# Token gathers of a 64-expert MoE layer issued five experts ahead, and seven output products of the first block placed behind the last down projection

## The reference

```
xn = layernorm(x)
x  = x + attention0(xn) + moe(xn)
xn = layernorm(x)
x  = x + attention1(xn) + ffn(xn)
```

## Time and profile before

| | us |
|---|---|
| median of 3 runs | 608.41 |
| lowest, highest | 607.96, 609.22 |
| the profiled execution | 609.91 |
| its span, first to last instruction | 607.8 |

### The profile page before, as it was taken

The page is one execution under the profiler, slowest core; times in us unless marked ns, Lnnn a source line. Parts: engine busy times, 40 slices in busy tenths (PEclk is TensorE's granted clock), DMA queues, the critical chain, the costliest instruction groups (busy, mean ns, idle before and its releaser), DMA issues.

```text
span 607.8 us, 9582 instructions
## 1 busy us (share of the span) xinstructions
PE 454.2 (75%) x2800; PEld 298.8 (49%) x2800; DVE 368.5 (61%) x960; ACT 200.1 (33%) x529; POOL 257.4 (42%) x237
## 2 busy tenths in 40 slices
PE   3846843287888888878878878889489989647866
PEld 1622513145455555545545545458234767536645
DVE  4999999544544444444443554532659867667984
ACT  1545220053334443343433334420165303021122
POOL 3331860215655665555665565632102043022444
PEclk9876985569888888898888999989689999788998
DMA  8430553628887878887887788733400287666502
GB/s 304 163 140 1 163 177 62 201 66 209 203 201 189 213 190 208 208 230 185 204 220 185 197 213 227 192 73 90 173 1 1 52 184 109 107 117 135 133 3 69
DMA packets 60579, 91.09 MB, mean 150 GB/s; under 512 B 23608, under 2 KB 39320, under 8 KB 60120
## 3 DMA queue, kind: packets, MB, share of 16 engines
q1 hardware_dynamic: 47656, 69.51, 41.0%
q0 software_dynamic: 12896, 21.24, 18.0%
HBM read 71.81 MB, written 18.12 MB: 148 GB/s over the span
## 4 chain that ended last, share of the span: by engine, by line
PE 26%; DMA 25%; issue 18%; DVE 15%; POOL 10%; ACT 4%; SPq 1%; ACTq 0%; POOLq 0%; DVEq 0%
PE ps L1431 19%; DMA big<-tok_tab,big 13%; DMA routed<-big 6%; POOL routed L655 6%; DMA big<-kr_dram 4%; POOL big L648 3%; DVE big L1409 3%; PE ps L1436 3%; DVE big L1046 2%; DVE big L1043 2%; DVE big L1050 1%; ACT big L810 1%; DMA big<-in_maa 1%; PE ps L1726 1%; PE ps L1743 1%
## 5 line engine op out<-in xcount | busy, mean ns | idle before, releaser
L1431 PE MATMUL ps<-big 128*128 128x352 f32 (+4 forms) x768 | 228.0, 448 | 2.3 <-ACT big L800 0.9
L1431 PEld LDWEIGHTS ps<-big 128*128 128x128 f32 (+2 forms) x768 | 150.9, 204 | 59.3 <-issue 23.8
L655 POOL DMA_INDIRECT routed<-big x64 | 101.8, 1591 | 127.2 <-ACT big L810 110.2
L648 POOL DMA_INDIRECT big<-tok_tab,big x64 | 63.5, 992 | 42.1 <-DVE big L1117 22.9
L1436 PE MATMUL ps<-cst,big 128*128 128x128 f32 x144 | 30.6, 301 | 57.9 <-DMA big<-tok_tab,big 56.5
L1139 DVE COPY big<-ps 88x256 f32<-88x256 f32 x64 | 26.9, 420 | 76.4 <-PE ps L1550 74.6
L1131 DVE SCALAR_TENSOR_TENSOR big<-big,ps 128x176 f32<-128x176 f32 x64 | 21.6, 338 | 78.3 <-ACT big L805 78.3
L1431 PE MATMUL ps<-xnT,big 128*128 128x512 f32 (+1 forms) x104 | 55.2, 690 | 14.8 <-ACT big L767 12.8
L800 ACT ACTIVATE big<-ps 128x256 f32<-128x256 f32 x64 | 24.5, 383 | 111.5 <-PE ps L1436 111.4
L1436 PEld LDWEIGHTS ps<-cst,big 128*128 128x128 f32 x144 | 17.7, 148 | 76.1 <-DMA big<-tok_tab,big 61.8
L1409 DVE TENSOR_TENSOR big<-ps,big 128x512 f32<-128x512 f32 x64 | 41.8, 677 | 9.3 <-PE ps L1726 9.3
(11 more groups left out here) (199 smaller groups left out, 679.7 us busy)
## 6 DMA issues: line engine op xcount, KB each, us to landing
big<-in_w SPq DMA_DIRECT2D x64, 352.0 KB
big<-in_w SPq DMA_DIRECT2D x64, 176.0 KB
big<-q_dram SPq DMA_DIRECT2D x144, 32.0 KB
big<-kr_dram SPq DMA_DIRECT2D x24, 192.0 KB
big<-kr_dram SPq DMA_DIRECT2D x72, 64.0 KB
big<-lo_tab SPq DMA_DIRECT2D x2, 2048.0 KB, 7.7
kr_dram<-big SPq DMA_DIRECT2D x12, 256.0 KB, 4.5
routed<-big POOLq DMA_DIRECT2D x2, 1152.0 KB, 14.1
```

The costliest lines, as they stand in the source:

```text
L648: nc.gpsimd.indirect_dma_start(xe[:, e % SLOTS, :], None, tok_tab, bass.IndirectOffsetOnAxis(ap=sidx[:, e:e + 1], axis=0))\
L655: nc.gpsimd.indirect_dma_start(routed[e % 2], bass.IndirectOffsetOnAxis(ap=sidx[:, e:e + 1], axis=0), ye[:, e % 2, :], None, compute_op=AL ...
L1431: last = nc.tensor.matmul(o, w, m, start=(n == 0), stop=(n == len(pairs) - 1))
```

## The change

- A small tile `gate_now` of 128x4 takes the gate column of each expert: `tokens_in` copies it on ACT ahead of its copy of the transposes, and `scale_out` reads it there. The slot of `xe` is so free once `tokens_in` of its expert is done.
- `token_gather(e)` therefore waits for `s_xeT` of expert e-4 and no longer for `s_y`. Five gathers are issued ahead of the loop, and in the loop `token_gather(e+5)` stands ahead of `routed_add(e)`.
- Of the output products only product 0 stays in the last group; products 1 to 7 follow the last down projection. DVE's adds are reordered around the additions of the `racc` halves, the statistics and the layernorm of half 0.
- SP issues the small rows of block 1 and `w5` ahead of the loads of `racc`, no longer behind them.

```diff
+        SLOTS = 4
+        gate_now = nat_tmp[:, 0, 0:SLOTS]
...
-        x1_at = [(), (), (0,), (1, 2, 3)]
+        x1_at = [(), (), (0,), ()]
...
             sp.wait_ge(s_lp, NG * 4)
+            sp.wait_ge(s_y, E + 1)
+            sp.dma_start(edrow, td_row.partition_broadcast(P)).then_inc(s_l1c, 16)
+            sp.dma_start(edcol, td_col).then_inc(s_l1c, 16)
+            sp.dma_start(urow, u_row.partition_broadcast(P)).then_inc(s_l1c, 16)
+            sp.dma_start(maat, maa).then_inc(s_l1c, 16)
+            sp.dma_start(w5, w_rkvgo).then_inc(s_w5, 16)
             for i in range(2):
                 sp.wait_ge(s_sc[i], 16 * (1 + E // 2))
                 for b in range(B):
                     sp.dma_start(racc[i][:, b * TPB:(b + 1) * TPB, :],
                                  routed[i][b * S:(b + 1) * S, :].rearrange("(t p) d -> p t d", p=P))\
                       .then_inc(s_racc[i][b], 16)
-            sp.wait_ge(s_y, E + 1)
-            sp.dma_start(w5, w_rkvgo).then_inc(s_w5, 16)
-            sp.dma_start(edrow, td_row.partition_broadcast(P)).then_inc(s_l1c, 16)
...
             def token_gather(e):
                 if e >= SLOTS:
-                    pool.wait_ge(s_y, e - SLOTS + 2)
+                    pool.wait_ge(s_xeT, e - SLOTS + 1)
...
-            for e in range(SLOTS):
+            for e in range(SLOTS + 1):
                 token_gather(e)
             for e in range(E):
+                if e + SLOTS + 1 < E:
+                    token_gather(e + SLOTS + 1)
                 routed_add(e)
-                if e + SLOTS < E:
-                    token_gather(e + SLOTS)
...
-            def tokens_in(e, u):
+            def tokens_in(e, u, gate):
                 act.wait_ge(s_xeTp, e + 1)
+                nc.scalar.activation(gate_now[:, u:u + 1], gate, ACT.Copy)
                 nc.scalar.activation(xeT[:, u % 2, :, :], PS[0][:, 0:D].rearrange("p (c n) -> p c n", c=DC),
                                      ACT.Copy).then_inc(s_xeT, 1)
...
-            def scale_out(e, u, free, gate):
+            def scale_out(e, u, free):
                 act.wait_ge(s_yp, e + 1)
+                act.wait_ge(s_xeT, e + 1)
                 act.wait_ge(s_sc[u % 2], free)
-                nc.scalar.activation(ye[:, u % 2, :], PS[3][:, 0:D], ACT.Copy, scale=gate).then_inc(s_y, 1)
+                nc.scalar.activation(ye[:, u % 2, :], PS[3][:, 0:D], ACT.Copy, scale=gate_now[:, u:u + 1])\
+                  .then_inc(s_y, 1)
...
-                        for t in range(3):
-                            x1_add(t)
+                        x1_add(0)
...
-            for t in range(3, TPB + 2):
+            for t in range(1, TPB):
                 x1_add(t)
-            dve.wait_ge(s_x1, TPB + 2)
+            dve.wait_ge(s_x1, TPB)
             routed_add(0, 0)
-            routed_add(0, 1)
+            x1_add(TPB)
             routed_add(1, 0)
             ln_stats(0)
-            for t in range(TPB + 2, NT):
+            for t in range(TPB + 1, TPB + 3):
                 x1_add(t)
-            dve.wait_ge(s_x1, NT)
-
+            ln_apply(1, 0)
             dve.wait_ge(s_ed, 2)
             note(nc.vector.tensor_scalar(edrow, edrow, 1e30, -1.0, ALU.min, ALU.mult))
             nc.vector.tensor_scalar(edcol, edcol, 1e30, -1.0, ALU.min, ALU.mult).then_inc(s_edn, 1)
-            ln_apply(1, 0)
+            x1_add(NT - 1)
+            dve.wait_ge(s_x1, NT)
+            routed_add(0, 1)
             routed_add(1, 1)
...
-            for t in range(4, NT):
+            for t in range(1, NT):
                 x1_product(t)
```

More of the change, by code:

```diff
@@ L421, in block_kernel @@
         LAST = NG - 1
-        x1_at = [(), (), (0,), (1, 2, 3)]
+        x1_at = [(), (), (0,), ()]
         oT_at = [(), (0, 1, 2), (3, 4, 5), (6, 7)]
-        SLOTS = 4
         KR_DMAS = PARTS + PARTS * PARTS
@@ L554, in _ @@
                       .then_inc(s_racc[i][b], 16)
-            sp.wait_ge(s_y, E + 1)
-            sp.dma_start(w5, w_rkvgo).then_inc(s_w5, 16)
-            sp.dma_start(edrow, td_row.partition_broadcast(P)).then_inc(s_l1c, 16)
-            sp.dma_start(urow, u_row.partition_broadcast(P)).then_inc(s_l1c, 16)
-            sp.dma_start(edcol, td_col).then_inc(s_l1c, 16)
-            sp.dma_start(maat, maa).then_inc(s_l1c, 16)
             sp.dma_start(gb[:, 0, :], gamma.partition_broadcast(P)).then_inc(s_gb, 16)
@@ L841, in unit @@
                 if g is not LAST or u + 2 < SLOTS:
-                    tokens_in(g * SLOTS + (u + 2), u)
-                scale_out(g * SLOTS + u, u, g * 32 + 16 * (1 + u // 2), gate)
+                    tokens_in(g * SLOTS + (u + 2), (u + 2) % SLOTS, gate)
+                scale_out(g * SLOTS + u, u, g * 32 + 16 * (1 + u // 2))
             def oT_copy(t):
@@ L853, in _ @@
             place_values(0, slice(0, 1), first=True)
-            tokens_in(0, 0)
+            tokens_in(0, 0, gates[:, 0, 0, 0:1])
             tanh(0, 0)
@@ L857, in _ @@
             exps(0, 1)
-            tokens_in(1, 1)
+            tokens_in(1, 1, gates[:, 1, 1, 0:1])
             with act.Fori(0, LAST) as g:
                 for u in range(SLOTS):
-                    unit(g, u, gates[:, u, u, bass.ds(g, 1)], bass.ds(g + 1, 1))
+                    n = (u + 2) % SLOTS
+                    unit(g, u, gates[:, n, n, bass.ds(g + (u + 2) // SLOTS, 1)], bass.ds(g + 1, 1))
             for u in range(SLOTS):
-                unit(LAST, u, gates[:, u, u, LAST:NG], None)
+                n = (u + 2) % SLOTS
+                unit(LAST, u, gates[:, n, n, LAST:NG], None)
             act.wait_ge(s_l1c, 64)
```

## The result

The changed kernel took 550.17 us in the median of 4 runs (548.33 to 556.54), against 608.18 us of the kernel before in the same runs: a ratio of 0.909, 95% interval 0.903 to 0.914. The direction was right, and its size was 34 us where 58 came.

The account below looks back on a forecast made before the run. Late gathers were taken to bound the expert loop, with DMA transfers next: 609.91 - 28.9 (loop) - 5 (end) = 576.0 us, less 1.5 for the median gives 574.5 us, range 557 to 598.

Parts of the forecast that it names:

- The gather ring: Expert loop: late gathers close a ring of four experts; issuing them earlier removes the gather wait entirely.
- Two experts more: POOL's queue in the loop: added gather lead of at least 2 x 3.2 us, against matmul waits of 2.6 at most.
- The transfers take over at a share of 0.92: 237 us: Expert loop: 218 us of full DMA share / 0.92 = 237 us, 28.9 us less.
- Rival 1: Expert loop: DMA share reaches 1.0 or over, only TensorE is left; 548 to 556 us in all; chance 0.11.
- Rival 2: Expert loop: uneven engines cap the mean DMA share at 0.84 to 0.88; 585 to 597 us in all; chance 0.20.
- Rival 3: Expert loop: scale_out waits for scatters landing in 6.7 us and over; 593 to 603 us in all; chance 0.06.
- rival 4: Loop gate copies cost 11 us while transfers already set the pace, end gives nothing back; about 618 us; chance 0.06.
- this floor: Loop scatters of one parity: scale_out(e) waits for scatter e-2 to land; 2.3 to 3.8 us an expert, 137 to 226 us.
- The end: 5 us: From the loop's end to block 1: first block-1 product 4.8 us earlier, taken as 5; bounds 1.7 to 8.
- the bound that I had worked out and put aside: SP queue at the end: w5, racc 0 and half 0, 2.9 MB, 11.8 us from 415.5, landing at 427.3.
- T: Landing of racc ring 1's half 0 load: forecast 424.2, before 427.75; first block-1 product then at T + 8.8.
- The clock rises: Expert loop: the mean clock rises above 0.92.

Follow-up runs that it names:

- the lead taken back: Changed kernel with the gather of e+4 behind the addition of e again, gate copies and new end kept: 611.29 us, ratio 1.011 against the kernel before.
- the three with late ones: The kernel before; that kernel with only the end reordered (606.32 us); the changed kernel with the gather of e+4 behind the addition of e (611.29 us).
- less work of TensorE: Changed kernel with half of each down product left out, 2 of 4 matmuls an expert: 551.95 us.
- fewer bytes: Changed kernel loading only 64 of the 512 columns of each w2 from the second group on: 547.51 us.
- the second one: Second profile of the changed kernel, run again unchanged on the chip of the other experiments: median 552.10 us.

## Why the prediction was wrong, point by point

1. *The gather ring bounds the loop, and its wait goes.* Right. With the lead taken back the loop is at 271 us, with it at 209 to 214.
2. *Two experts more lie between gather and use.* Right, and one would do.
3. *The transfers take over at a share of 0.92: 237 us.* This is the step that failed: 213.4 us measured, 23.6 less. (The total missed by 24.3: outside the loop 4 us of the extra gain were lost again, and the median lay 6.4 us below the profiled execution where 1.5 was assumed.) That they take over was right. The size was wrong in two ways. The share reached 0.96, and 0.98 over 38 us, above the 0.94 and 0.93 of the earlier trace rows, from which I even took a little off. And I took 0.82 x 265.86 = 218 us as a fixed amount of work. It is not: the same bytes (204 x 265.86 = 54.2 MB, 253 x 213.37 = 54.0 MB) took 0.96 x 213.37 = 205 us of full share after, 203 to 206 in the other loops with the same bytes and early gathers, but 218 to 220 in the three with late ones. With the share right and the 218 kept it would have been 218 / 0.96 = 227: 10 of the 24 us are the share, 14 the amount of work. Why the same bytes take less time of the engines is not shown. The stretches of the earlier trace rows gave 240 and 245 GB/s, and even from these alone it would have been 54.2 MB / 242 = 224 us.
4. *Rival 1, nothing but TensorE is left, 211 to 218 us and 548 to 556 in all.* Its numbers came true and its mechanism only in part: the share did rise to 0.96 and over, but TensorE was not all that was left, since less work of TensorE gave nothing and fewer bytes gave 6 to 10 us. That forecast and measurement meet in rival 1's total is in part luck. I gave it 0.11 because no long stretch before had a share over 0.94; but before, every such stretch ended in a hole of the kernel's own making, so the trace could not show a longer one.
5. *Rival 2, engines unevenly loaded, a cap at 0.84 to 0.88.* Wrong: the mean share was 0.96 to 0.98. The rule of the Trainium skill ("DMA: Bandwidth & Descriptors", "Why a DMA increments its semaphore by 16 and not by 1") on how many engines a narrow transfer uses was not tested by itself; if it holds here, it did not keep the mean down.
6. *Rival 3, late scatters, and rival 4, slower.* The output copy did wait for scatters, 10.2 us in 13 experts, which grew to 31.6 us in 28 with less TensorE, where it may be part of the bound. (By the earlier trace rows this floor is 2.2 to 3.7 us an expert, 134 to 224 us, not 137 to 226; nothing hangs on it.) Up to 6.8 us may be the gate copies where the gather is late, the piece of rival 4 that was real; in the changed kernel no cost of them could be seen, as the sum had it.
7. *The end: 5 us.* It was 2.5 us by the stages up to block 1 (-8.0 and +5.6). Scatter 63 came 1.5 us sooner than worked out (12.26 us behind scatter 60, for 13.8). But I let the load of half 0 land 3.85 us behind the scatter's landing; the queue set it, which was the bound that I had worked out and put aside: 13.7 us behind scatter 63 by that bound, 10.6 by the value taken, 15.2 measured. From T on the chain was right in this profile, T + 8.1 for T + 8.8 (T + 9.6 in the second one, at a clock of 0.65), and so was the new wait of x1_product(7) for VectorE.
8. *The clock rises.* Right: 0.92 to 0.99 in the loop, with 16 us less busy time for the same 957 matmul records.
9. *A measurement tells 0.2% from no change.* Wrong: the kernel before took 601.3 to 616.5 us over all runs, and the intervals of the ratios are 0.4% to 0.9% wide to either side.

## What to carry to other kernels

When a ring of latency is opened, the transfers that fill the holes can go faster than the mean of the trace with holes says, as here: work the new floor out from bytes and the best rate seen, not from the mean share times a guessed one, and put the case "the engines reach their full share" inside the range. A slot is free when its last reader is done: if that is a small part of the row (here one column of 320), copying it out early buys lead for the whole row, and the lead has to exceed the longest wait; here more of it gave nothing. And a load that is moved ahead in a queue is paid for by whatever stands behind it; here w5, needed much later, held the load that everything waited for back by 2.3 to 3.3 us, out of 8 that were won.

## What the runs showed of the hardware

The time that the 16 DMA engines spend on the same 54 MB is not constant. Over the stage from scatter 0 to scatter 60 the share times the length was 218 us before, 220 in both other kernels with late gathers, and 203 to 206 us in the kernels with the same bytes and early gathers. Nor does it follow the bytes: with 17% of them gone and the number of packets unchanged it was 187 us. With 8% more bytes in loads over 128 partitions the engines carried 265 GB/s at a share of 0.98, 8 to 12 GB/s more than the two profiles of the changed kernel show at 0.97 and 0.96.
